# Statistics matmuls issued one output group later in the product stages of a two-layer block

## The reference

```
x = x + layernorm(layernorm(x) @ weight.T + bias)
xf = layernorm(x)
probs = softmax(xf @ W_router.T); w = top-2 of probs, normalised
h = einsum('td,erd->ter', xf, lora_A)
lora = einsum('ter,eor,te->to', h, lora_B, w) * 2.0
x = x + layernorm(xf @ W_base.T + b_base + lora)
```

## Time and profile before

| | us |
|---|---|
| median of three timed runs | 3458.41 |
| lowest and highest of them | 3423.75, 3599.84 |
| the profiled execution | 3450.05 |
| its span (slowest core, core 7) | 3447.5 |
| spans of the other cores | 3384.8 to 3435.9 |

### The profile page before, as it was taken

One profiled execution on the slowest core, in us unless ns is written; L12 is line 12 of the kernel. 1 busy time (PEld: TensorE's weight loads), 2 busy tenths in 40 slices (PEclk: granted clock), 3 DMA queues, 4 the chain that ended last, 5 costly groups with the idle time before them and its releaser, 6 DMA issues.

```text
span 3447.5 us, 28233 instructions; the slowest of 8 cores (3384.8 to 3447.5 us)
## 1 busy us (share of the span) xinstructions
PE 2429.4 (70%) x10204; PEld 979.2 (28%) x10204; DVE 653.4 (19%) x1243; ACT 545.0 (16%) x1001; POOL 574.2 (17%) x777
## 2 busy tenths in 40 slices
PE   2688844888526995499824997299923999279990
PEld 0233312333202441144301442144400344034430
DVE  0400054000124004500034002700033100720003
ACT  3111120111031112111121112111122111201110
POOL 0011040100130113111130112311131111401104
PEclk7799966999757997599955998599965999578875
DMA  6399912999551431044242432033332343013322
GB/s 173 72 207 211 214 51 58 209 213 216 148 181 55 147 139 38 26 140 138 104 161 69 150 139 76 26 107 138 134 119 101 122 143 114 26 60 112 118 88 98
DMA packets 127975, 417.18 MB, mean 121 GB/s; under 512 B 12768, under 2 KB 12896, under 8 KB 127584
## 3 DMA queue, kind: packets, MB, share of 16 engines
q0 software_dynamic: 74336, 279.05, 30.6%
q1 hardware_dynamic: 36864, 102.78, 7.7%
q10 hardware_dynamic: 16640, 33.56, 3.0%
HBM read 383.98 MB, written 102.76 MB: 141 GB/s over the span
## 4 chain that ended last, share of the span: by engine, by line
PE 48%; DMA 24%; DVE 15%; issue 6%; ACT 3%; POOL 3%; DVEq 0%; ACTq 0%; POOLq 0%; SPq 0%
PE P L548 22%; PE P L358 19%; DMA wsc<-wbh 7%; DMA out<-ost 5%; DMA wbh<-wA 4%; DMA wbh<-wF 4%; DVE ybf L387 3%; DMA xt<-xT 3%; DVE ybf L436 3%; DVE ybf L274 3%; POOL ost L579 2%; DVE ybf L384 2%; PE ps_sq L320 1%; DVE ybf L573 1%; DVE ybf L576 1%
## 5 line engine op out<-in xcount | busy, mean ns | idle before, releaser
L358 PE MATMUL P<-u,wbh 128*128 128x512 bf16 x4096 | 977.8, 393 | 133.4 <-DVE u L277 79.8
L548 PE MATMUL P<-u,wbh 128*128 128x512 bf16 x4096 | 972.4, 398 | 58.6 <-DMA wbh<-wF 46.9
L358 PEld LDWEIGHTS P<-u,wbh 128*128 128x128 bf16 x4096 | 404.5, 100 | 697.7 <-issue 256.2
L548 PEld LDWEIGHTS P<-u,wbh 128*128 128x128 bf16 x4096 | 411.3, 102 | 604.9 <-issue 254.7
L311 POOL DMA_DIRECT2D wbh<-wsc x384 | 201.2, 528 | 1641.6 <-PE P L555 846.3
L338 ACT CAST zb<-P 128x512 bf16<-128x512 f32 x256 | 150.1, 586 | 2027.7 <-PE P L362 816.0
L189 DVE TENSOR_SCALAR row_zm<-ps_sq 1x512 f32<-1x512 f32 x8 | 5.4, 679 | 2173.1 <-PE ps_sqq L326 2173.1
L247 PE MATMUL ps_sq<-xbf,ones 128*1 128x512 bf16 x128 | 57.6, 547 | 347.6 <-ACT sq L239 347.6
L579 POOL TENSOR_TENSOR ost<-ybf,xt 128x512 f32<-128x512 bf16 x128 | 149.1, 1164 | 318.2 <-DVE ybf L576 318.2
L390 POOL TENSOR_TENSOR xt<-xt,ybf 128x512 f32<-128x512 f32 x128 | 153.8, 1202 | 165.7 <-DVE ybf L387 162.5
L339 ACT ACTIVATE sq<-P 128x512 bf16<-128x512 f32 x256 | 154.7, 604 | 0.0
(11 more groups left out here) (88 smaller groups left out, 1106.0 us busy)
## 6 DMA issues: line engine op xcount, KB each, us to landing
wbh<-wsc POOLq DMA_DIRECT2D x192, 544.0 KB, 4.7
wbh<-wsc POOLq DMA_DIRECT2D x192, 512.0 KB, 3.9
wsc<-wbh SPq DMA_DIRECT2D x64, 544.0 KB, 7.1
xt<-xT ACTq DMA_DIRECT2D x16, 2048.0 KB, 10.4
wsc<-wbh SPq DMA_DIRECT2D x64, 512.0 KB, 6.6
out<-ost SPq DMA_DIRECT2D x128, 256.0 KB, 2.4
wbh<-wA POOLq DMA_DIRECT2D x32, 544.0 KB, 11.9
wbh<-wF POOLq DMA_DIRECT2D x32, 544.0 KB, 11.7
```

Of the source, the lines that this page charges most:

```text
L358: t_run(lambda t, oc=oc, k=k, wt=wt: t.matmul(P[oc % 2][:], wt, u[:, k * C:(k + 1) * C], start=(k == 0), stop=False))
L548: t_run(lambda t, oc=oc, k=k, wt=wt: t.matmul(P[oc % 2][:], wt, u[:, k * C:(k + 1) * C], start=(k == 0), stop=False))
```

## The change

In each of the two product stages the batch for groups 4j to 4j+3 is emitted in the turn of group 4j+5 instead of group 4j+4, and ahead of the evacuation of group 4j+4 instead of behind that of group 4j+3. The eighth batch of a stage stays behind the loop. No instruction is added or removed.

```diff
@@ -363,9 +363,9 @@
                                               wbB[oc % 2][:, 16 * 128:17 * 128],
                                               onestile[:], start=False, stop=True))
                 if oc >= 1:
+                    if oc >= 2 and (oc - 2) % 4 == 3:
+                        emit_zstats_batch(oc - 2)
                     emit_evac(oc - 1, ch * 64)
-                    if (oc - 1) % 4 == 3:
-                        emit_zstats_batch(oc - 1)
             emit_evac(OC - 1, ch * 64)
             emit_zstats_batch(OC - 1)
             stats_b_done = t_pair[OC - 1]
```

## The result

| | before | changed |
|---|---|---|
| median of 10 runs, us | 3438.84 | 3516.09 |
| lowest run, us | 3408.04 | 3465.68 |
| profiled execution, us | 3450.05 | 3465.68 |

In some executions of either kernel the cores of one die, or of both, have a lower clock and the run is longer; five such runs of the changed kernel lift its median above 3500 (three of the ten before were such), and the ratio leaves them out. The ratio is 1.013, with a 95% interval of 1.0074 to 1.0187. So the change makes the kernel slower by some 1.3%, less than the 2% taken as the bound of a difference.

What follows compares the result with a forecast made beforehand. PE was taken to bound six product stages, weight transfers the two of chunk 0. The profiled 3450 us plus 60 (PE-bound stages), 0 (chunk 0) and 0 (clock) gave 3510 us, 1.7% more; range 3470 to 3560.

Steps and rivals of the forecast that it cites:

- The pause: Ahead of groups 6, 10, ...: ACT's copy and square lie open on PE, 1.71 us in place of 0.31.
- The 1.43 taken: Added time in us per moved batch in PE-bound stages, taken from two estimates, 1.40 and 1.45.
- The first reading: Around one moved batch: hand-overs, copy and square sum to 1.71 us in place of 0.31, 1.40 more.
- the end of the stage: Second estimate, from a stage's last, uncovered hand-over: 1.76 us against 0.31 covered, 1.45 more per batch.
- The PE-bound stages: Six product stages of chunks 1 to 3: 7 batches each at 1.43 us add 60 us.
- Chunk 0: Two transfer-bound product stages, 14 moved batches: 0 us added, since weight transfers fill some 0.9 of the time.
- The rival of exposed stages: Chunk 0: delayed loads let DMA queues run dry, costing 20 to 45 us, total 3530 to 3555; chance 0.17.
- The clock: Groups behind the new pauses: about 1.33 to 1.38 us of idle does not lower PE's clock; cost 0.
- The rival falls for this change: Groups 6, 10, ... in PE-bound stages: clock falls at every pause, 42 x 1.68 = 70 us more, 3581; chance 0.10.
- The reading of rows 8 and 9: Chunk 0 profile timelines: group undisturbed behind batch plus 1.40 us or 1.69 us alone, slowed behind batch plus 2.05 us.
- The kept clock: Core 7's last product stage: pauses keep its clock up, 34 us come back, 3476 (at the bound 3447); chance 0.12.
- The covered pause: At group 6 in PE-bound stages: PE would wait there anyway, so no cost, 3450 us; chance 0.03.

Runs made afterwards that it cites:

- e3: Changed kernel with eight square buffers instead of four, so ACT's work on group 4 waits for no batch; 0.9978 of before (0.9948 to 1.0008).
- e5: Changed kernel with ACT's wait for the batch moved from ahead of its copy to between copy and square; 1.0093 of before (1.0062 to 1.0123).
- e2: Kernel before with the batches late in chunk 0 only; 1.0004 of before (0.9984 to 1.0024).
- e6: Changed kernel with one more bank copy into an unused buffer in ACT's work on each group behind a batch; slowest profiled span 3510.9 us.
- e4: Kernel before, order kept, with eight square buffers instead of four; 0.9988 of before (0.9968 to 1.0008).
- e1: Kernel before with the batches late in chunks 1 to 3 only; 1.0157 of before (1.0122 to 1.0192).
- e11: Changed kernel with four more bank copies into unused buffers in ACT's work on each group behind a batch; slowest profiled span 3676.6 us.

## Why the prediction was right or wrong

The pause: right in place, cause and size. Forecast were 0.48 + 1.08 + 0.15 = 1.71 us from the batch's last matmul to group 6, measured 1.70 (0.47, 1.08, 0.15). The 1.43 taken was 0.05 too high: the cycle grew by 1.38. The first reading (1.40) was nearer than the end of the stage (1.45), where ACT starts 0.53 after the last matmul (1323.10, in the timeline) and not 0.47. Undoing ACT's wait (e3) and moving it behind the copy (e5) took away all and a third of the cost, so it is shown and not only argued.

The PE-bound stages: forecast 60 us, measured 58.

Chunk 0: forecast 0 between -25 and +45; measured +2.4 and -0.4 us, and 1.0004 for e2, -5 to +8 us. The rival of exposed stages (20 to 45) falls. The reason held in the main: the pause is open at most places, and in the second stage the waits for weights fall by as much. In the first they fall by less than the pauses add, within what executions differ by. That the transfers bound these stages was not tested by a run that changes them.

The clock: forecast 0, measured 0 slow groups of 336. The rule that matmuls should run back to back (Perfetto Trace Analysis of the Trainium skill, Matmul Optimizations), read without a limit, is not borne out at pauses of 1.32 and 1.81 us, and is at 2.10 and at about half the places with 2.30. The rival falls for this change; e6 shows that it was between 0.5 and 0.8 us away. The reading of rows 8 and 9 rested on the cores that were chosen: cores 4 and 5 of the same profile had a mean granted clock of 0.78 and 0.77 in the first stage, and there groups behind a batch took 8.4 us with no pause at all. Nor does 2.05 us bound it: core 6 of that profile has groups of 6.9 us behind pauses of 2.22 and 2.41.

The kept clock: no core of the changed kernel had its last stage at 0.83 in its profile, but none had in those of e2 to e4 either, with PE in chunks 1 to 3 as dense as before. The rival's price of 34 us was too small: its two stretches also hold time outside the stage, and core 7's stages alone are 300.9 and 252.9 us, 48 apart (and the range begins at 3470, not at the 3476 that the price gives). So what touched cores 6 and 7 in the profile before was that execution's, and nothing shows that the pauses spared it. Whether pauses can do that was not tried.

The covered pause falls: PE waits at all 42 places.

The time: 3510 was forecast, and the median was 3516.09, but this agreement is luck. The median is the middle between the fifth and the sixth of ten runs, 3484.16 and 3548.01, and no run lies near it: five runs of the changed kernel lie at 3466 to 3484, around the lower end of the range, and five at 3548 and above. The term of the sum that was off is its base, the profiled execution of 3450.05, which the text compared with the median but not with the other cores. Core 7's last stage was 48 us longer at the low clock than the others' (300.9 and 253.0); the quickest six cores had spans of 3385 to 3411. From those, 3411 + 2.5 + 60 gives 3473, amid the lower five. The ratio of 1.013 holds the 58 us (1.017) within its interval, and e1's 1.0157, with the same pauses in chunks 1 to 3, stands nearer to it. The call of a slowdown inside 2% was right.

## What to carry to other kernels

Before moving an instruction later on one engine, look up what it releases on the others. Here the batch released a buffer that ACT needed before it could empty a bank, and the bank was wanted by the very next thing on PE. A wait that costs nothing (506 us of them on ACT) says only that there was distance behind it; where an order is changed, each such wait has to be priced with its new distance, and more buffers (e3) buy the distance back. Where the sum starts from a profiled execution, compare its slowest core with the others first.

## What the runs showed that was not expected

The share of groups that start at the low clock behind a pause does not grow steadily with the pause. At the usual pauses of 1.32, 1.81, 2.30, 2.79 and 3.28 us the five kernels have 0, 8, 177, 91 and 253 slow groups of 336, and the 8 stand behind pauses of 2.10 us, not of 1.81. Which batches they stand behind repeats from core to core.

A slow group behind a pause costs one of two amounts, with little between: mostly about 1.7 us (8.6 in place of 6.9; 8.2 to 8.6 in all), and in 164 of the 253 cases of e11 mostly 2.9 us (9.8; 9.2 to 9.9).

In chunk 0, which the transfers bound, the late order left the second stage no longer and perhaps a few us shorter, while it cost 9.5 to 9.9 us in every stage bound by PE.
